# Two-piece table loads, 128-partition ids and one output row in a DLRM tower kernel

## What is computed

```
e = stack([tbl_f[ids[:, f]] for f in range(26)], axis=1)          # 512 x 26 x 128
combined = concatenate((dense[:, None, :], e), axis=1)            # 512 x 27 x 128
interactions = einsum('bfd,bgd->bfg', combined, combined)
z = concatenate((dense, upper triangle of interactions), axis=1)  # 128 + 351
h = concatenate([z, dense], axis=1)                               # 607
h = maximum(h @ W_top1 + b_top1, 0)                               # 512 x 512
h = maximum(h @ W_top2 + b_top2, 0)                               # 512 x 256
y = h @ W_top3                                                    # 512 x 1
```

## Time and profile before

| what | value |
|---|---|
| median of 3 runs | 168.21 us (164.83 to 168.46) |
| span of the profiled execution, first to last instruction | 161.2 us |
| PE, DVE, ACT, POOL busy | 100.3, 56.4, 59.5, 67.7 us |
| moved by DMA | 16.47 MB, 102 GB/s on the mean |

### The profile page before, as it was taken

The page is one execution under the profiler, slowest core; times in us unless marked ns, Lnnn a source line. Parts: engine busy times, 40 slices in busy tenths (PEclk is TensorE's granted clock), DMA queues, the critical chain, the costliest instruction groups (busy, mean ns, idle before and its releaser), DMA issues.

```text
span 161.2 us, 3493 instructions
## 1 busy us (share of the span) xinstructions
PE 100.3 (62%) x1477; PEld 85.9 (53%) x1477; DVE 56.4 (35%) x128; ACT 59.5 (37%) x84; POOL 67.7 (42%) x72
## 2 busy tenths in 40 slices
PE   5349395938094580097769269687999769019800
PEld 5226273726073450075558259576899769019700
DVE  0064554846155304365755322050611342000200
ACT  3113272453270701356082723496455532001000
POOL 4778777777777777604772710720000000000000
PEclk9999959999959789569969969999999999855895
DMA  1454444457875444433442112223131022000000
GB/s 44 128 184 157 156 158 156 160 178 204 225 215 159 143 147 159 154 133 139 142 159 64 35 37 83 59 72 97 49 97 45 4 74 67 0 0 4 0 0 0
DMA packets 8239, 16.47 MB, mean 102 GB/s; under 512 B 2553, under 2 KB 3689, under 8 KB 8143
## 3 DMA queue, kind: packets, MB, share of 16 engines
q1 hardware_dynamic: 6144, 11.98, 22.4%
q0 software_dynamic: 2080, 4.26, 10.0%
HBM read 14.75 MB, written 1.50 MB: 101 GB/s over the span
## 4 chain that ended last, share of the span: by engine, by line
DMA 39%; PE 20%; SPq 19%; ACT 10%; issue 4%; DVE 2%; ACTq 0%; DVEq 0%
DMA table_raw<-tbl 32%; PE gram_bank L458 6%; PE layer_bank L485 6%; DMA pairs<-pair_scratch 6%; ACT emb L588 5%; SPq L351 4%; PE layer_bank L504 4%; SPq L347 3%; SPq L340 2%; SPq L349 2%; ACT table_hi L565 2%; PE unit_bank L425 2%; SPq L308 2%; SPq L345 2%; SPq L302 2%
## 5 line engine op out<-in xcount | busy, mean ns | idle before, releaser
L394 POOL DMA_INDIRECT rows<-tbl,gather_ids x65 | 66.9, 1029 | 37.2 <-issue 18.6
L425 PE MATMUL unit_bank<-onehot,table_hi 125*128 125x512 f32 (+1 forms) x80 | 30.0, 534 | 33.0 <-issue 16.5
L425 PEld LDWEIGHTS unit_bank<-onehot,table_hi 125*128 125x128 f32 x80 | 20.1, 265 | 40.0 <-issue 26.7
L635 DVE TENSOR_SCALAR onehot<-shifted_ids 125x512 fp32r<-125x512 f32 (+1 forms) x80 | 28.8, 429 | 22.6 <-ACT shifted_ids L557 22.6
L565 ACT CAST table_hi<-table_raw 125x1024 fp32r<-125x1024 f32 (+1 forms) x11 | 10.6, 967 | 42.0 <-DMA table_raw<-tbl 42.0
L425 PE MATMUL unit_bank<-onehot,table_lo 125*128 125x512 f32 (+1 forms) x80 | 21.0, 407 | 0.0
L643 DVE TENSOR_TENSOR table_lo<-table_raw,table_hi 125x1024 fp32r<-125x1024 f32 x10 | 12.2, 1225 | 24.6 <-ACT table_hi L565 24.6
L485 PE MATMUL layer_bank<-pairs,w_pairs 117*128 117x128 f32 x96 | 14.5, 315 | 7.1 <-DMA pairs<-pair_scratch 7.1
L425 PEld LDWEIGHTS unit_bank<-onehot,table_lo 125*128 125x128 f32 x80 | 16.8, 211 | 3.8
L485 PEld LDWEIGHTS layer_bank<-pairs,w_pairs 117*128 117x128 f32 x96 | 13.6, 227 | 7.3 <-DMA pairs<-pair_scratch 7.2
L458 PE MATMUL gram_bank<-emb 128*27 128x27 f32 x960 | 11.8, 200 | 8.5 <-ACT emb L588 5.6
(11 more groups left out here) (29 smaller groups left out, 50.7 us busy)
## 6 DMA issues: line engine op xcount, KB each, us to landing
table_raw<-tbl SPq DMA_DIRECT2D x9, 500.0 KB
match_ids<-onehot_ids SPq DMA_DIRECT2D x10, 250.0 KB
pair_scratch<-gram_rows SPq DMA_DIRECT2D x3, 364.5 KB
rows<-tbl,gather_ids POOLq DMA_INDIRECT x65, 4.0
w_pairs<-w_pairs SPq DMA_DIRECT2D x1, 702.0 KB
w_dense_parts<-w_dense SPq DMA_DIRECT2D x1, 512.0 KB
w_sb<-w SPq DMA_DIRECT2D x1, 512.0 KB, 9.5
table_raw<-tbl SPq DMA_DIRECT2D x2, 250.0 KB
```

The costliest lines, as they stand in the source:

```text
L394: pool.indirect_dma_start(rows[:, t % 2, slot - 1, :], None, tables[table], bass.IndirectOffsetOnAxis(ap=gather_ids[:, t, table:table + 1] ...
L425: last = nc.tensor.matmul(bank[:, 0:served], part[:, i % 2, c * D:(c + 1) * D], onehot[:, i % 2, c, 0:served], start=(c == 0 and part is t ...
L635: nc.vector.tensor_scalar(onehot[:, i % 2, c, 0:served], shifted_ids[:, i % 2, 0:served], float(c), None, ALU.is_equal) \
```

## The change

Each table load becomes two transfers, of the first 112 partitions and of the last 13, which add to the same semaphore; who waits for the table waits for 32 in place of 16. The ids are broadcast to 128 partitions, of which ACT reads 125. In layer 3 the two operands change places, so a tile's result is a row of 128 values on one partition; `y_sb` is one row of 512 values, and SP stores it once, when all four tiles are done.

```diff
--- before.py
+++ after.py
@@ -49,6 +49,8 @@
 ONEHOT_ROWS = 1000
 ONEHOT_CHUNKS = 8
 ONEHOT_PARTS = ONEHOT_ROWS // ONEHOT_CHUNKS
+EVEN_PARTS = ONEHOT_PARTS // 16 * 16
+PART_PIECES = [slice(0, EVEN_PARTS), slice(EVEN_PARTS, ONEHOT_PARTS)]
 NH = len(ONEHOT_TABLES)
 
 SLOT_FEATURES = [0] + [t + 1 for t in range(TABLES) if t not in ONEHOT_TABLES]
@@ -201,7 +203,7 @@
         dense_sb = sb("dense_sb", [P, BATCH])
         rows = sb("rows", [P, 2, GATHERED[0], D])
         gather_ids = sb("gather_ids", [P, TILES, TABLES], I32)
-        match_ids = sb("match_ids", [ONEHOT_PARTS, NH, BATCH], I32)
+        match_ids = sb("match_ids", [P, NH, BATCH], I32)
         RAW = 3
         table_raw = sb("table_raw", [ONEHOT_PARTS, RAW, ONEHOT_CHUNKS * D])
         table_hi = sb("table_hi", [ONEHOT_PARTS, 2, ONEHOT_CHUNKS * D], F32R)
@@ -223,7 +225,7 @@
         b2_sb = sb("b2_sb", [P, N2_BLOCKS])
         hidden1 = sb("hidden1", [P, N1_BLOCKS, P])
         hidden2 = sb("hidden2", [P, N2_BLOCKS, P])
-        y_sb = sb("y_sb", [P, TILES])
+        y_sb = sb("y_sb", [1, BATCH])
 
         def psum(name):
             return ctx.enter_context(nc.psum_tensor(name, [P, 512], F32))
@@ -251,7 +253,7 @@
 
 
         gram_piece_bank = gram_bank + unit_bank
-        y_psum = layer2_bank[0][:, P:P + 1]
+        y_psum = layer2_bank[0][0:1, P:2 * P]
 
         ids_loaded = sem("ids_loaded")
         dense_loaded = sem("dense_loaded")
@@ -300,12 +302,13 @@
 
                 eng.wait_ge(lo_ready, i - RAW + 1)
             eng.dma_start(match_ids[:, i, :],
-                          onehot_ids[i:i + 1, :].to_broadcast([ONEHOT_PARTS, BATCH])) \
+                          onehot_ids[i:i + 1, :].to_broadcast([P, BATCH])) \
                .then_inc(match_ids_loaded[i], 16)
             source = tables[ONEHOT_TABLES[i]].rearrange("(p c) d -> p (c d)", c=ONEHOT_CHUNKS)
 
             for half, loaded in zip(table_pieces(i), (table_loaded[i], second_half_loaded)):
-                eng.dma_start(table_raw[:, i % RAW, half], source[:, half]).then_inc(loaded, 16)
+                for parts in PART_PIECES:
+                    eng.dma_start(table_raw[parts, i % RAW, half], source[parts, half]).then_inc(loaded, 16)
 
         def store_pairs(eng, j):
 
@@ -367,10 +370,9 @@
                 for read in PAIR_READS[1:]:
                     load_pairs(sp, t, TILE_REGIONS[t], read).then_inc(pairs_loaded[t], 16)
 
-            for t in range(TILES):
-                sp.wait_ge(y_copied, t + 1)
-                sp.dma_start(out[t * P:(t + 1) * P, :], y_sb[:, t:t + 1]).then_inc(out_stored, 16)
-            sp.wait_ge(out_stored, 16 * TILES)
+            sp.wait_ge(y_copied, TILES)
+            sp.dma_start(out.rearrange("n one -> one n"), y_sb[:, :]).then_inc(out_stored, 16)
+            sp.wait_ge(out_stored, 16)
 
         @block.gpsimd
         def _(pool):
@@ -510,7 +512,7 @@
             def fill_layer3(t):
                 for m in range(N2_BLOCKS):
                     pe.wait_ge((hidden2_act, hidden2_dve)[m], t + 1)
-                    last = nc.tensor.matmul(y_psum, hidden2[:, m, :], w3_sb[:, m:m + 1],
+                    last = nc.tensor.matmul(y_psum, w3_sb[:, m:m + 1], hidden2[:, m, :],
                                             start=(m == 0), stop=(m == N2_BLOCKS - 1))
                 last.then_inc(y_filled, 1)
 
@@ -554,14 +556,14 @@
 
                     act.wait_ge(onehot_ready, ONEHOT_CHUNKS * (i - 1))
                 served = BATCH - ONEHOT_FROM[i] * P
-                nc.scalar.activation(shifted_ids[:, i % 2, 0:served], match_ids[:, i, BATCH - served:BATCH],
+                nc.scalar.activation(shifted_ids[:, i % 2, 0:served], match_ids[0:ONEHOT_PARTS, i, BATCH - served:BATCH],
                                      ACT.Identity,
                                      bias=minus_first_row[:, 0:1]).then_inc(shifted_ready, 1)
                 if i >= 2:
 
                     act.wait_ge(unit_filled, unit_of[("onehot", i - 2)] + 1)
                 for half, loaded in zip(table_pieces(i), (table_loaded[i], second_half_loaded)):
-                    act.wait_ge(loaded, 16)
+                    act.wait_ge(loaded, 16 * len(PART_PIECES))
                     nc.scalar.copy(table_hi[:, i % 2, half], table_raw[:, i % RAW, half]).then_inc(hi_ready, 1)
 
             act.wait_ge(first_row_ready, 1)
@@ -636,9 +638,9 @@
                                             float(c), None, ALU.is_equal) \
                              .then_inc(onehot_ready, 1)
 
-                dve.wait_ge(table_loaded[i], 16)
+                dve.wait_ge(table_loaded[i], 16 * len(PART_PIECES))
                 if i == 0:
-                    dve.wait_ge(second_half_loaded, 16)
+                    dve.wait_ge(second_half_loaded, 16 * len(PART_PIECES))
                 dve.wait_ge(hi_ready, i + 2)
                 nc.vector.tensor_tensor(table_lo[:, i % 2, :], table_raw[:, i % RAW, :],
                                         table_hi[:, i % 2, :].bitcast(F32), ALU.subtract) \
@@ -681,7 +683,7 @@
                 elif step[0] == "layer3":
                     t = step[1]
                     dve.wait_ge(y_filled, t + 1)
-                    nc.vector.tensor_copy(y_sb[:, t:t + 1], y_psum).then_inc(y_copied, 1)
+                    nc.vector.tensor_copy(y_sb[:, t * P:(t + 1) * P], y_psum).then_inc(y_copied, 1)
 
 
 def kernel(**inputs):
```

## The result

The changed kernel took 151.57 us (median of 4 runs, 149.34 to 153.11) against 167.19 us of the kernel before in the same group of runs (164.83 to 168.46): a ratio of 0.911, 95% interval 0.898 to 0.925. It is faster, and the sign was forecast with a chance of 0.96; but 119.3 us was forecast, and 151.57 lies outside the range of 115 to 131. Medians are over all runs of a kernel, and ratios with their intervals over its undisturbed runs alone, so the two need not divide exactly.

A forecast was written before the change was run, and what follows sets the result against it. Table loads on few DMA engines were taken as the bound, with PE, POOL's gathers and the tail behind. Span 161.2 - 34.9 - 6.2 - 2.65 - 5.3 + 0.1 = 112.3, + 7.0 = 119.3 us; range 115 to 131.

The forecast's parts named there:

- Step 1: Table and id loads: spread over more DMA engines, 4.5 us per table, gram of tile 0 at 51.5 us, not 91.76.
- Step 2: POOL's gathers then set gram of tile 3, at 91.4 us, 34.9 us earlier than 126.33.
- The slack of 5.3 us: One-hot stage: would be ready at 86.1 us against 91.4 by the gathers, so up to 5.2 us per table cost nothing.
- Step 3: Tail: without early y stores, tile 3's pair loads land 6.2 us earlier, and layer 1 at full clock saves 2.65 us.
- Step 4: Last store of y: one 2 KB row lands in 2.2 us, not 7.5, a gain of 5.3 us.
- The term outside the span: Time added to the profiled span to get the run time: 7.0 us, or 3.6 by the fastest run.
- steps 3 to 5: Tail: earlier pairs and full clock, one store of y, and small things costing 0.1 us; 14.05 us gained together.
- B: Rival: gathers or one-hot stage fall behind the sum, 122 to 131 us; chance 0.2.
- A: Rival: tile 3's pair loads are slow in themselves, 8.85 us of gain falls away, 128.1 us; chance 0.2.
- C: Rival: the table split doesn't spread over engines and only the tail gains, 154.2 us; chance 0.08.
- D: Rival: SP is blocked by its own issues, up to 5.78 us each, so slower, 203 us; chance 0.03.

The follow-up runs named there:

- groups 4 and 5: Two sets of runs, kernels taking turns with the kernel before on one chip; the whole change took 119.11 and 122.34 us, the kernel before 164.03 and 163.33.
- groups 1 and 3: Two sets of runs beside the kernel before (166.31 and 165.68 us); row of y alone 152.89 and 150.97, whole change 152.84 in the second.
- groups 2 and 4: Two sets of runs in which the kernel before took 162.84 and 164.03 us; the whole change took 119.11 in the second and was not run in the first.

## Why the prediction was right or wrong

- **Step 1 failed in the result, in its pace per table.** The loads did what was said (share about 1, waits for tables down from 41.9 to 3.3 us). But "With the waits between the engines I take 4.5 us per table once the loads are early" took PE's products to be seen when they end, and to follow one another. In the result's execution they did not, with up to 8.5 us of ACT's idle at a time, and gram of tile 0 came at 84.5 and not at 51.5. Nothing in the trace of before points to it: its ACT idles 1.9 us in all before these copies.
- **In groups 4 and 5 step 1 failed by its rate.** Taken were 281 GB/s, share 1 in place of 0.70 at 197; measured were 258, 243 and 227 GB/s at a share of 1.03 to 1.05. And 226 GB/s over the first 54 us are 12.2 MB, not "some 11": the tenth table and POOL's later gathers share the queues. 11 MB at 281 are 39 us, 12.2 at 226 are 54: gram of tile 0 at 63.4. "The upper rate, since nothing but the share was short" was the wrong choice; at a full share the rate per share was lower than at 0.70.
- **Step 2 held** where PE was prompt: without later tables gram of tile 3 at 91.6 and 92.3. Where the one-hot stage was last instead, its own rule, 34.6 us from gram of tile 0, gives 98.0 and 98.1 in groups 4 and 5, measured 100.2 and 99.1. The slack of 5.3 us was used up. In the result 84.5 + 34.6 would be 119.1, and 128.4 was measured: the lateness goes on.
- **Step 3 held in size** (layer 1 at 2.2 us after the issue, clock at 1.0; y late alone gave 5.9 us), and its reason is half of the truth.
- **Step 4** was sized too small: 0.9 us and not 2.2 for the store, so a gain of 6.7 us and not 5.3.
- **The term outside the span was wrong.** The forecast added 7.0 us, the median of one set of runs less the span of another execution. Every run on record has 1.8 to 2.4 us outside its span, so the trace of 161.2 us belongs to an execution of about 163 us, faster than each of the three runs beside it. With 1.8 in its place the same steps give 114.1 us, below the stated range.
- **The sum in the result.** Gram of tile 3 is 128.4 and not 91.4, + 37.0, of which 33.0 had come by gram of tile 0; the tail is 19.1 and not 20.9, - 1.8; outside the span are 1.8 us and not 7.0, - 5.2. Together 119.3 + 30.0 = 149.3, the time of the profiled execution.
- **The sum in group 4.** Gram of tile 3 is 100.2, + 8.8; the tail is 18.9, - 2.0; outside the span are 1.9, - 5.1. Together 119.3 + 1.7 = 121.0, the time of that execution. That the forecast of 119.3 met the median of 119.11 us is therefore luck: errors of opposite sign cancel. In group 5 it was 3 us short. For the row alone steps 3 to 5 forecast a gain of 14.05 us; 16.1 was measured in group 4.
- **The rivals.** B is what groups 4 and 5 show in part (late one-hot stage), and 122.34 lies within its 122 to 131. A and C are refuted, since the pairs landed in 2.2 us and the split spread. D is too: in groups 4 and 5 the changed kernel's issues beside the weights took up to 2.1 and 3.9 us, most others 0.35 to 1.7, not 5.78 each. None of them names the lateness, and that is the real gap: every rival was a resource of the kernel. (D's threshold of 4.2 us per issue comes out as 4.1 when its own sum is redone.)

What the lateness is stays open: the runs show where the time goes, and not what causes it. Shown is this. It comes and goes with the group, not with the kernel alone: the row alone has it in groups 1 and 3 and not in 4, the changed kernel in the result and group 3 and not in 4 and 5, the tables alone in 1 and not in 5. It is no matter of the chip's number: groups 1 and 4 share it. It didn't go with the fullness of the DMA engines. Nor were the packets slower by which instructions are loaded: the 12 of 16 KB took 0.9 to 1.4 us each in the result's trace and in that of the changed kernel in group 4 alike; whether they were asked for late isn't shown. The kernel before has none in its three traces, the one ahead of the prediction and those of groups 2 and 4, but it was never traced in a group with the lateness, and its medians there are 165.7 to 167.2, else 162.8 to 164.0: it may have some too, hidden for the most part behind its waits for tables. Traces with the lateness hold only 1005 to 1189 semaphore events, those without 2011 to 2309 (1623 with few gathers). The profile infers from these events what ended an idle time, so "issue" and "remote" in the traces with the lateness can stand for a releaser that wasn't recorded. What records the execution may even have a part in the lateness; that was not tried. Gains by the loads are thus 0 in one kind of group and 29 us more than the row's in the other (147.94 against 119.11).

## What to carry to other kernels

Look at the partition count of every load, for with 125 rows the mean share of the DMA engines was 0.32 and with 112 + 13 it was about 1; but when the share goes to 1, take the rate from a row that is already full, since it fell from 281 expected to 226 to 258 GB/s, and what stands first in the queues then decides which engine waits. When a load is moved back in a queue, look for who works in order behind it: here ACT carried the wait to a gram matrix that didn't need the load. Store a result as one row, once, at the end: 2 KB in one row landed in 0.9 us, 128 pieces of 4 bytes in 5.3 to 8.3, and the latter can delay the completion of loads ahead of them. When a measured gain is 30 us short of the sum, and the traces show idle time that no wait of the program explains, run the same kernel in a second group before explaining it.

## What was not expected of the hardware

- PE's products one at a time, 0.7 to 2.8 us apart with nothing waited for, and ACT idle up to 8.5 us in the result's trace (13.6 us for the row alone in group 3, 20.6 us for the cut at 100 rows) before it copied products; in the last case PE's last product had ended 17 us before the copy.
- Loads whose packets had moved by 138 us and whose completion was seen at 144.4, seen only with the early small stores and both kinds of load over 125 rows.
- A share of the DMA engines of 1.03 to 1.05 with anything from 217 to 258 GB/s. What sets the rate at a full share was not tried.
